# A perceiver block on one core: instruction order around the second layer norm, v apart from q and k, the quantiser's scaled value moved to VectorE

## The reference, cut to what matters

```
xn   = layernorm(x);  C = ctx @ Wkv_d                         # cross attention, 16 heads
s    = ((xn @ Wq_d @ W_qk) per head) . C / sqrt(32);  x2 = x + softmax(s) @ (C @ Wv_u)
q,k,v = layernorm(x2) @ Wqkv + bqkv                           # self attention, one head of 128
x3   = x2 + softmax(q k' / sqrt(128)) @ v @ Wo + bo
h    = layernorm(x3) @ hadamard;  step = max(max|h|, 1e-5)/7  # quantised feed-forward, per row
y    = x3 + (clip(round(h/step), -8, 7) * step) @ ternary(weight)'
```

## Time and profile before

| what | value |
|---|---|
| median of three runs | 356.9 us (356.89, 359.89, 356.90) |
| the profiled execution's own time | 358.43 us |
| its span, first to last instruction | 356.6 us |
| PE busy | 308.3 us (86%), 4612 matmuls |
| PE weight load busy | 203.9 us (57%) |
| DVE busy | 251.1 us (70%), 530 instructions |
| ACT busy | 191.7 us (54%), 629 instructions |
| POOL busy | 93.1 us (26%), 133 instructions |
| mean granted TensorE clock | 0.960 of 2.4 GHz |
| chain that ended last | PE 35%, DVE 25%, ACT 24%, issue 11%, POOL 2% |
| transfers | 25.37 MB, mean 71 GB/s |

### The profile page before, as it was taken

How to read it: one execution, slowest core, us unless ns; L and a number is a source line. 1 busy time by engine, 2 the same in 40 slices (tenths; PEclk the granted TensorE clock), 3 DMA queues, 4 the chain that set the end, 5 groups by cost and what they waited for, 6 DMA issues and landing times.

```text
span 356.6 us, 11424 instructions
## 1 busy us (share of the span) xinstructions
PE 308.3 (86%) x4612; PEld 203.9 (57%) x4612; DVE 251.1 (70%) x530; ACT 191.7 (54%) x629; POOL 93.1 (26%) x133
## 2 busy tenths in 40 slices
PE   5766759999798999899999999999999999968871
PEld 3445447665456566666666565657575666645520
DVE  1454883878587787778787878788787878767432
ACT  1360652847547483829384756657484839282210
POOL 2004232323212221314132323222222223131321
PEclk9995687999999999999999999999999999998997
DMA  7980210303113130303040312213132020000000
GB/s 219 332 304 2 67 54 8 113 4 93 56 35 119 33 118 31 118 29 118 3 141 3 102 45 51 96 29 118 31 119 63 2 61 2 33 2 31 0 31 29
DMA packets 13345, 25.37 MB, mean 71 GB/s; under 512 B 3200, under 2 KB 3712, under 8 KB 13312
## 3 DMA queue, kind: packets, MB, share of 16 engines
q1 hardware_dynamic: 13312, 24.91, 21.5%
HBM read 20.71 MB, written 4.19 MB: 70 GB/s over the span
## 4 chain that ended last, share of the span: by engine, by line
PE 35%; DVE 25%; ACT 24%; issue 11%; POOL 2%; DMA 1%; POOLq 0%; DVEq 0%; ACTq 0%
ACT prob L313 11%; DVE mx L435 10%; PE ps L716 9%; PE ps L612 6%; PE ps L722 5%; PE ps L730 4%; DVE nmx L439 3%; ACT prob L310 3%; PE ps L737 3%; DVE stat L464 3%; DVE stat L483 3%; PE ps L706 2%; POOL rstd L267 2%; ACT q_t L301 2%; ACT p2t L301 2%
## 5 line engine op out<-in xcount | busy, mean ns | idle before, releaser
L310 ACT ACTIVATE prob<-ps,nmx,qk_scale 128x128 f32<-128x128 f32 x128 | 56.7, 457 | 39.5 <-DVE nmx L439 39.5
L622 PE MATMUL ps<-had_s,x3t 128*128 128x512 f32 x128 | 59.2, 606 | 1.4 <-ACT x3t L301 1.4
L313 ACT ACTIVATE prob<-ps,nmx,qk_scale 128x128 f32<-128x128 f32 x128 | 48.5, 489 | 0.0
L435 DVE TENSOR_REDUCE mx<-ps 128x8 f32<-128x1024 f32 x32 | 39.0, 1220 | 10.0 <-PE ps L612 10.0
L445 DVE STREAM_TRANSPOSE prob_t<-prob 128x1024 f32<-128x1024 f32 x32 | 39.1, 1223 | 6.9 <-ACT prob L313 6.9
L294 POOL TENSOR_TENSOR res<-prod,x 128x512 f32<-128x512 f32 x16 | 20.2, 1264 | 82.0 <-DVE prod L549 82.0
L622 PEld LDWEIGHTS ps<-had_s,x3t 128*128 128x128 f32 x128 | 23.0, 190 | 27.2 <-issue 25.3
L655 PEld LDWEIGHTS ps<-x2t,wqkv_s 128*128 128x128 f32 x256 | 30.9, 198 | 10.4 <-ACT x2t L301 10.4
L716 PE MATMUL ps<-prob_t,ckv_n 32*32 32x128 f32 x2048 | 33.1, 300 | 4.0 <-DVE prob_t L445 2.5
L655 PE MATMUL ps<-x2t,wqkv_s 128*128 128x128 f32 x256 | 33.9, 288 | 2.9 <-ACT x2t L301 1.4
L259 POOL TENSOR_TENSOR rstd<-aux,power 128x1 f32<-128x1 f32 x16 | 8.8, 548 | 91.5 <-DVE aux L470 91.5
(11 more groups left out here) (112 smaller groups left out, 559.7 us busy)
## 6 DMA issues: line engine op xcount, KB each, us to landing
ct<-ctx_cols SPq DMA_DIRECT2D x16, 512.0 KB, 4.0
xt<-x_cols SPq DMA_DIRECT2D x16, 256.0 KB, 2.7
xr<-x_rows SPq DMA_DIRECT2D x16, 256.0 KB, 2.7
y<-res SPq DMA_DIRECT2D x16, 256.0 KB, 3.6
w_rows<-weight SPq DMA_DIRECT2D x1, 1024.0 KB, 7.9
had_s<-hadamard SPq DMA_DIRECT2D x1, 1024.0 KB, 7.0
wqkv_s<-wqkv SPq DMA_DIRECT2D x1, 768.0 KB, 8.3
wqk<-w_qk SPq DMA_DIRECT2D x2, 128.0 KB, 4.5
```

The lines of the kernel that those rows point to most:

```text
L310: last = nc.scalar.activation(prob[:, h, :], score, ACT.Exp, bias=nmx[:, h:h + 1], scale=scale, accum_out=sum_a[:, h:h + 1])
L313: last = nc.scalar.activation(prob[:, h, :], score, ACT.Exp, bias=nmx[:, h:h + 1], scale=scale)
L435: V.tensor_reduce(mx[:, h], ps[:, 2 * half:2 * half + 2, :].rearrange("p r (c k) -> p (r c) k", c=EC), AX.X, ALU.max).then_inc(done["mx"], 1)
L622: mm = pe.matmul(ps[:, B4, :], x3t[:, c, :], had_s[:, c, :], start=(c == 0), stop=(c == EC - 1))
```

## The change

It reorders three engines and moves one operation; no product is added or dropped.

- DVE: second norm's statistics (stat2 to aux2) come straight behind x2, ahead of any maximum. The maximum is taken in three pieces instead of two (heads 0 to 3, 4 to 7, 8 to 15), the last behind the third norm's statistics. z is computed on DVE (PSUM source) behind qinv, with qi right behind it, both ahead of `turned(0)`; the tile `round_c` goes. mx2 and nmx2 come ahead of qi_t. x3 comes right behind `turned(1)`, and prod last.
- ACT: without z. Heads 0 to 3, x2t, heads 4 and 5, lat, heads 6 and 7, q and k, heads 8 to 10, **p2, v, p2t, heads 11 and 12, o2t, heads 13 to 15**, q_t, ckv, u_t.
- PE: s, had, x2t, both halves of lat, q and k (own semaphore), qt, s2, qi transposes, v (own semaphore), p2t, half the integer product, o2t, the other half, wo, ckv, u, x3t, xo. The integer product was in two halves before as well.
- Iterations 0 and 1: const_row moves from ahead of `turned(0)` to the end of iteration 0, ternary is split over the end of iteration 0 and iteration 1, and scale_row is made in iteration 1.

```diff
-                def largest(half):
...
-                    h = slice(8 * half, 8 * half + 8)
...
+                def largest(n, r0, r1):
...
+                    h = slice(4 * r0, 4 * r1)
+                    V.tensor_reduce(mx[:, h], ps[:, r0:r1, :].rearrange("p r (c k) -> p (r c) k", c=EC),
...
-                if cross:
-                    after(dve, made["s"], i)
-                    largest(0)
-                if self_:
                     after(dve, read["xo"], i - 1)
...
                 if cross:
-                    largest(1)
-                if isinstance(i, int) and i == 0:
-                    dve.wait_ge(ld_w["b"], 64)
-                    V.tensor_copy(bv_wide[:], b_qkv[:, 2:3].to_broadcast([P, P])).then_inc(bvw_done, 1)
-                    ternary_scale()
-                    dve.wait_ge(cb_made, 1)
-                    V.tensor_tensor(const_row[:], ps[:, B4, :], bo_row[:], ALU.add).then_inc(const_ready, 1)
-                if isinstance(i, int) and i == 1:
-                    ternary()
+                    after(dve, made["s"], i)
+                    largest(0, 0, 1)
+                    largest(1, 1, 2)
...
+                if cross:
+                    largest(2, 2, 4)
+                if isinstance(i, int) and i == 0:
+                    dve.wait_ge(ld_w["b"], 64)
+                    V.tensor_copy(bv_wide[:], b_qkv[:, 2:3].to_broadcast([P, P])).then_inc(bvw_done, 1)
+                    ternary_scale()
+                if isinstance(i, int) and i == 1:
+                    ternary((2, 3))
+                if quant:
...
+                    after(dve, done["qinv"], i - 2)
+                    V.tensor_scalar(z[:], ps[:, B4, :], qinv[:], ROUND, ALU.mult, ALU.add).then_inc(read["had"], 1)
+                    after(dve, read["had"], i - 2)
+                    V.tensor_scalar(qi[:], z[:], ROUND, QMAX, ALU.subtract, ALU.min).then_inc(done["qi"], 1)
...
-                if quant:
-                    after(dve, read["had"], i - 2)
-                    V.tensor_scalar(qi[:], z[:], ROUND, QMAX, ALU.subtract, ALU.min).then_inc(done["qi"], 1)
...
                     V.tensor_scalar(nmx2[:], mx2[:], -float(D2) ** -0.5, None, ALU.mult).then_inc(done["nmx2"], 1)
+                if quant:
+                    after(dve, made["qit"], i - 2)
+                    V.tensor_scalar(qi_t[:], qit_bank.rearrange("p (c t) -> p c t", c=EC), QMIN, None, ALU.max)\
+                        .then_inc(read["qit"], 1)
+                if self_:
+                    after(dve, done["exp2"], i - 1)
+                    after(dve, read["wo"], i - 2)
+                    V.reciprocal(rsum2[:], sum2[:]).then_inc(done["rsum2"], 1)
                 if cross:
                     turned(1).then_inc(made["pt"], 1)
+                if self_:
...
+                    V.scalar_tensor_tensor(x3[:, 1 - par], ps[:, B3, :], rsum2[:], x2b[:], ALU.mult, ALU.add)\
+                        .then_inc(read["wo"], 1)
                 if cross:
                     after(dve, done["rsum"], i - 1)
                     V.tensor_reduce(sum_a[:, 8:16], prob[:, 8:16, :], AX.X, ALU.add).then_inc(done["sum"], 1)
+                if quant:
...
+                if isinstance(i, int) and i == 0:
+                    dve.wait_ge(cb_made, 1)
+                    V.tensor_tensor(const_row[:], ps[:, B4, :], bo_row[:], ALU.add).then_inc(const_ready, 1)
+                    ternary((0, 1))
                 if cross:
                     after(act, made["pt"], i - 1)
                     after(act, done["rsum"], i - 1)
-                    after(act, done["nmx"], i * 2)
-                    exps(0, 6)
+                    after(act, done["nmx"], i * 3)
+                    exps(0, 4)
                 if self_:
                     after(act, made["x2t"], i - 1)
                     copy(x2t[:], ps[:, B2, :].rearrange("p (c t) -> p c t", c=EC)).then_inc(read["x2t"], 1)
+                if cross:
+                    after(act, done["nmx"], i * 3 + 1)
+                    exps(4, 6)
...
-                if quant:
-                    act.wait_ge(ld_w["wq"], 16)
-                    after(act, done["qinv"], i - 2)
-                    after(act, done["qi"], i - 3)
-                    nc.scalar.activation(z[:], ps[:, B4, :], ACT.Identity, bias=round_c[:], scale=qinv[:])\
-                        .then_inc(read["had"], 1)
-                if cross:
-                    after(act, done["sum"], i - 1)
-                    after(act, done["nmx"], i * 2 + 1)
-                    exps(8, 11)
-                if self_:
-                    after(act, made["qkv"], i - 1)
+                if self_:
...
-                    after(act, made["o2t"], i - 2)
-                    copy(v2[:], ps[:, B1, 2 * P:3 * P]).then_inc(read["qkv"], 1)
-                if cross:
-                    exps(11, 16).then_inc(done["exp"], 1)
+                if cross:
+                    after(act, done["sum"], i - 1)
+                    after(act, done["nmx"], i * 3 + 2)
+                    exps(8, 11)
                 if self_:
                     after(act, done["nmx2"], i - 1)
                     after(act, done["rsum2"], i - 2)
...
-                if self_:
+                if self_:
+                    after(act, made["v"], i - 1)
+                    after(act, made["o2t"], i - 2)
+                    copy(v2[:], ps[:, B1, 2 * P:3 * P]).then_inc(read["v"], 1)
                     after(act, made["p2t"], i - 1)
...
                     last.then_inc(read["p2t"], 1)
+                if cross:
+                    exps(11, 13)
+                if self_:
                     after(act, made["o2t"], i - 1)
                     after(act, made["wo"], i - 2)
                     copy(o2t[:], ps[:, B3, 0:P]).then_inc(read["o2t"], 1)
+                if cross:
+                    exps(13, 16).then_inc(done["exp"], 1)
+                if front:
...
                 if first and i == 1:
-                    hadamard_mean()
+                    wide_scale()
+                if self_ and quant:
...
+                    mm.then_inc(made["x2t"], 1)
                 if front:
...
-                    for s in range(3):
+                    for s in range(2):
                         for c in range(EC):
-                            w, xc = wqkv_s[:, c, s * P:(s + 1) * P], x2t[:, c, :]
-                            mm = pe.matmul(ps[:, B1, s * P:(s + 1) * P], w if s < 2 else xc, xc if s < 2 else w,
...
-                    mm.then_inc(made["qkv"], 1)
-                if quant:
-                    after(pe, done["qi"], i - 2)
...
-                    mm.then_inc(made["qit"], 1)
+                    mm.then_inc(made["qk"], 1)
...
-                if front:
-                    if self_:
-                        after(pe, read["qkv"], i - 1)
-                    pe.matmul(ps[:, B1, 0:2 * SKV], fold4[:].rearrange("p r l -> p (r l)"), lat[:, P:P + 2 * SKV],
-                              start=True, stop=True).then_inc(made["ckv"], 1)
...
-                if self_:
+                if quant:
+                    after(pe, done["qi"], i - 2)
+                    for c in range(EC):
+                        mm = pe.transpose(qit_bank[:, c * P:(c + 1) * P], qi[:, c * P:(c + 1) * P], ident_b[:])
...
+                    mm.then_inc(made["v"], 1)
                     pe.wait_ge(ld_w["wq"], 16)
...
                     mm.then_inc(made["p2t"], 1)
                 if quant:
+                    after(pe, read["qit"], i - 2)
+                    for c in range(2):
+                        pe.matmul(ps[:, B4, :], qi_t[:, c, :], tern_t[:, c, :], start=(c == 0), stop=False)
+                if self_:
+                    after(pe, read["v"], i - 1)
...
+                    after(pe, read["o2t"], i - 1)
+                    pe.matmul(ps[:, B3, :], o2t[:], wo_s[:], start=True, stop=True).then_inc(made["wo"], 1)
+                if front:
+                    if self_:
+                        after(pe, read["v"], i - 1)
+                    pe.matmul(ps[:, B1, 0:2 * SKV], fold4[:].rearrange("p r l -> p (r l)"), lat[:, P:P + 2 * SKV],
+                              start=True, stop=True).then_inc(made["ckv"], 1)
+                if first and i == 0:
+                    wide_bias()
...
-                if self_:
-                    after(pe, read["o2t"], i - 1)
-                    pe.matmul(ps[:, B3, :], o2t[:], wo_s[:], start=True, stop=True).then_inc(made["wo"], 1)
+                if first and i == 1:
+                    ternary_transposed(1)
+                if self_:
+                    if front:
+                        after(pe, read["qt"], i + 1)
+                    after(pe, read["wo"], i - 1)
+                    for c in range(EC):
+                        mm = pe.transpose(ps[:, B2, c * P:(c + 1) * P], x3[:, 1 - par, c * P:(c + 1) * P], ident[:])
+                    mm.then_inc(made["x3t"], 1)
                 if cross:
                     if front:
```

(42 more changed lines are left out.)

95 lines of the change are left out of this document (42 added, 53 removed).

## The result

The changed kernel takes **395.8 us** (median of 4) against 357.6: ratio 1.106, interval 1.098 to 1.113. The forecast was 383 with a range of 366 to 395: the sign held, the size did not, and the range missed by 0.8. The profiled execution's span is 393.8 us against 356.6.

What follows compares the result with a forecast made beforehand. No engine is full (TensorE 86% busy), so order and waits decide. Periods of 20.75 + 0.5 + 0.25 = 21.5 us give +31.6; ends +0.6, -4.4, -1.2: 385.0, lowered to 383 us for the profiled execution; range 366 to 395.

Steps and rivals of the forecast that it cites:

- part 1: VectorE's list from xm to nmx2: ends at 12.19 against 12.66 before, a gain of only 0.5 us a period.
- part 2: From nmx2 to the next xm: ScalarE's heads 11 to 15 wait behind p2; 8.55 us against 6.2.
- part 4: TensorE's clock falling to 1.2 GHz for some us: 0.25 us a period, bounds 0 and 0.7.
- Wo, x3t and ckv are off this path: Between p2 and the next xm: these are done beside heads and u_t, which gives back 1.7 us.
- part 3: GpSimd's x2b beside VectorE holds the third nmx: 0.5 us a period taken, bounds 0 and 0.85.
- GpSimd's start would wander more than the 0.2: x2b against the third nmx: GpSimd's start moves by more than the deciding 0.2, so 0.5 was taken, not 0.85.
- the clock falling in every period: Rival: u, p2t, o2t and had at 1.2 GHz, about 1.1 us more a period, 396 us; chance 0.08.
- part 5: Start and end iterations: -4.4 from const_row in iteration 0, iteration 1 at 0, iteration 15 +0.6, iteration 16 -1.2.
- VectorE is not last: Rival: nmx2 is there when ScalarE is through head 10; 18.85 a period, 348 us in total; chance 0.11.

Runs made afterwards that it cites:

- mx2 early: Kernel after with mx2 and nmx2 ahead of turned(0) on VectorE and qi_t right behind turned(0): 364.3 us, ratio 1.018 to the kernel before.
- the extra matmuls: Kernel after with six more matmuls, which nothing reads, on TensorE ahead of v in its idle stretch: 394.5 us, ratio 1.101 to the kernel before.
- the start's moves alone: Kernel before with only the change's work of iterations 0 and 1 (const_row, ternary, scale_row): 350.2 us, ratio 0.976.
- v ahead of the qi transposes: Kernel after with mx2 and nmx2 ahead of turned(0), x2b behind qk_scale, and v ahead of the qi transposes on TensorE: 351.6 us, ratio 0.982.
- Heads first: Kernel after with heads 11 to 15 listed on ScalarE ahead of p2: 391.2 us, ratio 1.094 to the kernel before.
- x2b late: Kernel after with x2b moved behind qk_scale on GpSimd: 380.3 us, ratio 1.062 to the kernel before.

## Why the prediction was right or wrong

- *VectorE's list (part 1).* Right. Forecast 12.20 to p without contention; with x2b out of the way 12.30 on average. Z took 0.75, the upper bound, where 0.69 was taken; the maximum of four heads took 0.68, where 0.69 was taken. P waited 2.94 to 3.37 for nmx2, 1.9 was forecast; x2b makes up most of the difference.
- *ScalarE's order (part 2).* The mechanism was right and is shown from both sides: p2 ahead of five heads costs 2.62 a period in the kernel before, and mx2 early gives 2.35 back in the kernel after. With the clock kept at full by the extra matmuls, `turned(1)` comes 3.44 after p and u 4.83; 3.51 and 4.82 were forecast. **The step that failed is in here and in part 4: "Wo, x3t and ckv are off this path".** X3t is. Wo and ckv are only at full clock, as long as the heads hold `turned(1)`. At 1.2 GHz they took 2.08 and 1.06, together 3.14 instead of 1.83, and in eight of thirteen periods TensorE came last, by 0.53 in the one shown. In the other five the low clock delayed `turned(1)` itself. U started 5.19 to 5.77 after p.
- *GpSimd beside VectorE (part 3).* The term was mis-sized: 0.5, measured 0.85 to 1.0. The third nmx took 1.08 to 1.24 in all thirteen periods, and moving x2b away shortened the first half by 0.92. The Trainium skill ("SBUF — State Buffer", Who interferes with whom) says that of a VectorE pass using both ports and a GpSimd pass the first to start holds the ports for its whole instruction. The trace agrees, nmx ending 0.02 to 0.04 after x2b, and I should have priced it by that. That GpSimd's start would wander more than the 0.2 was the false part: both times hang on the same aux3.
- *TensorE's clock (part 4).* Mis-sized: 0.25, with bounds of 0 and 0.7. The second half averages 9.37 (22.59 less 13.22), 8.80 was forecast with that term. The level of 1.2 GHz came in every period, and taking it away by itself gives 0.61 over iterations 4 to 13; the second half is then 8.67, 8.55 being forecast without the term. So the clock cost 0.6, inside the bounds. I gave the clock falling in every period 0.08 as a rival at 396. Its condition came true and the time is there, but the time partly by luck: its 1.1 a period is nearly twice what the clock cost, and x2b made up the rest. Nor does 1.1 give 396: added to the forecast it gives 397.7, in place of the 0.25 it gives 394.5.
- *The ends (part 5).* The start gained more: 51.72 against 59.80 for xm of iteration 2, -8.1, forecast -4.4. Up to xm of iteration 1 the forecast was right: 30.05 against 34.48, -4.4. There is some luck in that, for the start's moves alone give 5.4 there (29.04). The rest is iteration 1, 21.67 against 25.32, which was taken as 0. The start's moves alone bring xm of iteration 2 to 53.44, and with the second norm ahead of the first maximum to 51.52, so nearly all of the gain comes from these two together, about 1.9 of it from the norm, which part 5 doesn't count. Iteration 15 +0.8 (0.6 forecast), what follows -1.2 (-1.2).

By the spans: 13 x (22.59 - 19.07) = 45.7, -8.1, +0.8, -1.2: 37.2, the measured difference. Forecast were 31.6, -4.4, +0.6, -1.2. The 10.6 between them are 14.1 in the periods, halved over the first half (13.22 against 12.70: x2b, z) and the second (9.37 against 8.80: the clock), and 0.2 in iteration 15, less the start's 3.7. The forecast median is 12.8 too low and not 10.8, because 385.0 was lowered by 1.5 for the profiled execution and 383.5 put down as 383.

Three readings of the prediction were slightly off, and none decides. Stat3 adds up to 4.48 after xm, not 4.44. The copies of p2t start 0.08 after TensorE's p2t ends in the earlier trace rows, not 0.04. From the end of u_t's copy to xo has 0.26, not 0.10; the kernel after has 0.14.

Of the rivals, "VectorE is not last" is ruled out by the waits: p waited for nmx2 in all 16 pairs. What stays open is why TensorE stops inside u in some iterations of some versions. The moves of q, k and v into two groups, and of wo and ckv ahead of u, were not tried by themselves.

## What to carry to other kernels

A wait costs what stands behind it in its engine's queue, so compare the time of the awaited result with the moment the engine gets there, before work that other engines need is put behind the wait. Where two paths end within about half a microsecond, taking away either shows little (here 0.33 and 0.61 of 1.56 a period); remove both before calling one harmless. Read the part of a change that sits outside the loop by itself: here it was worth 8 us, and the loop hid it.

## What was not expected of the hardware

- TensorE worked at 1.2 GHz for a stretch of every period of the kernel after, while it was busy 85% of the time (249.94 of 293.62) and its longest idle stretch was 2.28 us (2.03 in most periods). Giving that stretch six matmuls that nobody reads kept the clock at 1.00 in iterations 4 to 13 and made the period 0.6 shorter.
- A VectorE pass over 8 columns took 1.08 to 1.24 instead of 0.23 beside a GpSimd sum of two SBUF tiles, each time GpSimd had started 0.05 to 0.22 earlier. The same pass over 4 columns, which started 0.1 ahead of GpSimd's x2n, kept its 0.23.
- TensorE can stop in the middle of u's 128 matmuls without a wait that the trace shows: for 1.47 us in iteration 3 of the kernel before, 1.07 in iteration 3 of the kernel after, 1.62 there with mx2 early, 1.82 with v ahead of the qi transposes, and twice with the extra matmuls alone (1.83 and 1.85). Heads first has no such stop, nor has x2b late. These are single profiled executions, and the cause is not known.
